# A mixture-of-experts block: eight output buffers, expert numbers read earlier, a two-part list

## The reference

```python
weights, indices = _gate(xt, gate_w)                    # 4 of 16 experts for each token
combine = jnp.einsum('tk,tke->te', weights, jax.nn.one_hot(indices, E, dtype=weights.dtype))
h1 = jnp.einsum('td,eid->tei', xt, W1)
h3 = jnp.einsum('td,eid->tei', xt, W3)
g = jax.nn.silu(h1) * h3 * combine[:, :, None]
y = jnp.einsum('tei,edi->td', g, W2)
z = jax.nn.silu(xt @ Ws1.T) * (xt @ Ws3.T) @ Ws2.T      # the shared expert
return (y + z).reshape(shape)
```

## Time and profile before

| | us |
|---|---|
| median of 3 runs (990.09, 994.32, 994.60) | 994.32 |
| the profiled execution, its own time | 992.58 |
| its span, first to last instruction | 990.8 |
| PE busy in the span | 867.0 |
| DVE busy | 732.7 |
| POOL busy | 658.6 |
| ACT busy | 573.9 |

### The profile page before, as it was taken

The page is one execution under the profiler, slowest core; times in us unless marked ns, Lnnn a source line. Parts: engine busy times, 40 slices in busy tenths (PEclk is TensorE's granted clock), DMA queues, the critical chain, the costliest instruction groups (busy, mean ns, idle before and its releaser), DMA issues.

```text
span 990.8 us, 19931 instructions
## 1 busy us (share of the span) xinstructions
PE 867.0 (88%) x6994; PEld 736.1 (74%) x6994; DVE 732.7 (74%) x1589; ACT 573.9 (58%) x1072; POOL 658.6 (66%) x625
## 2 busy tenths in 40 slices
PE   5688999999999999999999997738887899999940
PEld 5556777878878888788888786637775799999940
DVE  5777999987978788787888885585765466666648
ACT  1345777778887877887887886622321244444410
POOL 3555878978797888888788886515666555555530
PEclk9999999999999999999999999958997899999975
DMA  8661613223423235222325136233223333434337
GB/s 299 233 134 31 178 32 83 62 56 87 150 50 84 56 87 172 58 69 52 89 57 160 41 99 229 85 83 108 90 98 130 120 116 116 120 118 122 108 123 302
DMA packets 65757, 111.20 MB, mean 112 GB/s; under 512 B 16917, under 2 KB 43292, under 8 KB 63820
## 3 DMA queue, kind: packets, MB, share of 16 engines
q1 hardware_dynamic: 46905, 69.24, 26.4%
q10 hardware_dynamic: 11843, 22.84, 6.5%
q0 software_dynamic: 6912, 17.84, 4.9%
HBM read 46.06 MB, written 39.58 MB: 86 GB/s over the span
## 4 chain that ended last, share of the span: by engine, by line
PE 57%; DVE 11%; DMA 11%; POOL 11%; issue 5%; ACT 3%; SPq 0%; POOLq 0%; ACTq 0%; DVEq 0%
PE bank L691 12%; PE bank L693 10%; PE bank L692 10%; DMA slots<-h,slot_i 8%; PE bank L871 7%; PE bank L1087 7%; POOL p_lo L1927 5%; PE bank L848 4%; POOL turns L1905 2%; PE bank L1059 2%; PE bank L945 2%; DVE nmax L1261 2%; POOL slots L1983 1%; DVE qk L1241 1%; DVE turns L1235 1%
## 5 line engine op out<-in xcount | busy, mean ns | idle before, releaser
L1927 POOL TENSOR_TENSOR p_lo<-p_f,p_hi 128x512 f16<-128x512 f32 x256 | 329.5, 1299 | 46.2 <-ACT p_f L1662 45.2
L1659 ACT ACTIVATE p_hi<-bank,log_up 128x512 f16<-128x512 f32 x256 | 176.3, 689 | 108.0 <-PE bank L693 99.1
L1261 DVE TENSOR_REDUCE nmax<-bank 128x1 fp32r<-128x512 f32 x256 | 174.4, 685 | 84.4 <-PE bank L848 81.3
L1662 ACT ACTIVATE p_f<-bank,log_up 128x512 f32<-128x512 f32 x256 | 175.4, 685 | 14.7 <-POOL p_lo L1927 14.7
L871 PEld LDWEIGHTS bank<-vals,p_hi 128*128 128x128 f16 x2048 | 110.5, 98 | 59.2 <-POOL p_lo L1927 27.7
L871 PE MATMUL bank<-vals,p_hi 128*128 128x66 f16 x2048 | 138.8, 194 | 14.8 <-POOL p_lo L1927 14.5
L1905 POOL TENSOR_TENSOR turns<-turns 128x512 f32<-128x512 f32 x64 | 90.9, 1423 | 65.9 <-DVE turns L1235 65.9
L1241 DVE TENSOR_TENSOR qk<-rows_f,qk 128x512 fp32r<-128x512 f32 (+1 forms) x128 | 132.7, 1037 | 2.2
L691 PE MATMUL bank<-qk 128*128 128x512 f32 x256 | 122.2, 477 | 6.0 <-issue 4.8
L871 PE MATMUL bank<-vals,p_lo 128*128 128x66 f16 x1024 | 121.2, 193 | 0.0
L848 PE MATMUL bank<-qk 128*128 128x512 f32 x256 | 104.4, 411 | 3.6 <-DVE nmax L1261 3.2
(11 more groups left out here) (231 smaller groups left out, 2091.8 us busy)
## 6 DMA issues: line engine op xcount, KB each, us to landing
rows_f<-turns SPq DMA_DIRECT2D x64, 256.0 KB, 3.9
slots<-pad ACTq DMA_DIRECT2D x4, 2880.0 KB, 10.1
xs<-slots SPq DMA_DIRECT2D x80, 144.0 KB
w_hi<-parts SPq DMA_DIRECT2D x16, 512.0 KB, 8.4
rows_f<-kl_f SPq DMA_DIRECT2D x32, 192.0 KB, 3.0
w_raw<-in_w ACTq DMA_DIRECT2D x4, 1408.0 KB, 11.8
h_dram<-h_hl SPq DMA_DIRECT2D x3, 1024.0 KB, 4.9
qk<-lat_st SPq DMA_DIRECT2D x16, 192.0 KB, 4.3
```

The source lines that it names most:

```text
L1261: dve.tensor_reduce(nmax[:, k % MAXES:k % MAXES + 1], max_bank[q % 2][:], AX_X, ALU.max, negate=True)\
L1659: act.activation(p_hi[:, u % TB, :], score_bank[u % 2][:], ACT.Exp, bias=log_up[:, 0:1], scale=SCALE)
L1662: act.activation(p_f[:, u % 2, :], score_bank[u % 2][:], ACT.Exp, bias=log_up[:, 0:1], scale=SCALE)\
L1927: pool.tensor_tensor(p_lo[:, u % TB, :], p_f[:, u % 2, :], p_hi[:, u % TB, :], ALU.subtract).then_inc(s_pl, 1)
```

## The change

Three things.

Outputs and destinations have OUTS = 8 buffers. `ys` is now a list of eight slices: the four of before, two of `gate`'s first row, two of `zg`; `sel_i` has eight columns, and `e_put` eight semaphores. ACT and DVE wait for a landed scatter only from tile 8. The loads `xs` and `sel` keep four buffers. POOL's scatters take the same eight, and SP's last wait is for eight semaphores instead of four.

PE reads the first packed numbers ahead of shared position 14 (`t == NT - 2`), waiting there for `listed`; the waits for all weights (`w_h`, `w_l`, `ld_w2`) stand before the first routed inner product, no longer ahead of the transposes.

The list is made in two parts: `pack_experts` (behind t = 6), which subtracts one and packs, and `experts_of_tiles` (behind t = 8), which writes `own_i` and `sent_for`. `owners` goes to t = 2 and 4.

```diff
-        sel_i = sb("sel_i", [P, CYCLE], U32)
+        sel_i = sb("sel_i", [P, OUTS], U32)
...
-        ys = spare.rearrange("p (j n) -> p j n", j=CYCLE)
+        ys = [xa[:, j, :] for j in range(TB)] + [gate[:, 0, j, :] for j in range(2)] + [zg[:, j, :] for j in range(2)]
...
-            for t in range(NT):
-                shared_position(t, t % 2)
-
-
-            pe.wait_ge(listed, 1)
-            pe.wait_ge(w_h, 1 + E)
-            pe.wait_ge(w_l, 1 + E)
-            pe.wait_ge(ld_w2, 48)
-
...
+            for t in range(NT):
+                if t == NT - 2:
+                    pe.wait_ge(listed, 1)
+                    first_numbers = expert_numbers(0)
+                shared_position(t, t % 2)
...
                     expert = experts[place + 2]
+                    if m == 0:
+                        pe.wait_ge(w_h, 1 + E)
+                        pe.wait_ge(w_l, 1 + E)
+                        pe.wait_ge(ld_w2, 48)
                     pe.wait_ge(e_lo, m + 1)
...
-                if t in (3, 7):
-                    owners(t // 4)
-                if t == 11:
+                if t in (2, 4):
+                    owners(t // 2 - 1)
+                if t == 6:
+                    pack_experts()
+                if t == 8:
                     experts_of_tiles()
...
-                    if not (static(m) and m < CYCLE):
-                        dve.wait_ge(e_put[jm], 16 * over(m, CYCLE))
-                    dve.tensor_copy(sel_i[:, jm:jm + 1], sel[:, jm, 1:2]).then_inc(e_idx, 1)
+                    jo = m % OUTS
+                    if m >= OUTS:
+                        dve.wait_ge(e_put[jo], 16 * over(m, OUTS))
+                    dve.tensor_copy(sel_i[:, jo:jo + 1], sel[:, jm, 1:2]).then_inc(e_idx, 1)
...
-                    if not (static(n) and n < CYCLE):
-                        act.wait_ge(e_put[j], 16 * over(n, CYCLE))
-                    act.activation(ys[:, j], y_bank[j % 2][:, 0:D], ACT.Copy).then_inc(e_yc, 1)
+                    if n >= OUTS:
+                        act.wait_ge(e_put[n % OUTS], 16 * over(n, OUTS))
+                    act.activation(ys[n % OUTS], y_bank[j % 2][:, 0:D], ACT.Copy).then_inc(e_yc, 1)
```

More of the change, by code:

```diff
@@ L64 @@
 PACK = CYCLE + 2
-assert SLOT_TILES % CYCLE == 0 and E ** PACK <= 2 ** 24
+OUTS = 8
+assert SLOT_TILES % OUTS == 0 and SLOT_TILES % CYCLE == 0 and E ** PACK <= 2 ** 24
 R_KEEP = 0
@@ L333, in program @@
         sel = sb("sel", [P, CYCLE, 2])
-        sel_i = sb("sel_i", [P, CYCLE], U32)
+        sel_i = sb("sel_i", [P, OUTS], U32)
         h2_flat = h2[:].rearrange("p t n -> p (t n)")
         xs = sb("xs", [P, CYCLE, XW])
-        ys = spare.rearrange("p (j n) -> p j n", j=CYCLE)
+        ys = [xa[:, j, :] for j in range(TB)] + [gate[:, 0, j, :] for j in range(2)] + [zg[:, j, :] for j in range(2)]
+        assert len(ys) == OUTS
         sent_for = modT2[:].rearrange("p w c b -> p (w c b)").bitcast(I32)
@@ L400, in program @@
         ld_s = [sem(f"ld_s{j}") for j in range(CYCLE)]
-        e_put = [sem(f"e_put{j}") for j in range(CYCLE)]
+        e_put = [sem(f"e_put{j}") for j in range(OUTS)]
         ld_y = [sem(f"ld_y{j}") for j in range(PARTS_AHEAD)]
@@ L668, in _ @@
             expert_steps(sp, load_slots)
-            for j in range(CYCLE):
-                sp.wait_ge(e_put[j], 16 * (SLOT_TILES // CYCLE))
+            for j in range(OUTS):
+                sp.wait_ge(e_put[j], 16 * (SLOT_TILES // OUTS))
             sp.wait_ge(e_g, SLOT_TILES)
@@ L1090, in expert_position @@
                     mm.then_inc(e_y, 1)
-            expert_steps(pe, expert_position, expert_numbers)
+            expert_steps(pe, expert_position, lambda first: expert_numbers(first) if first else first_numbers)
         @block.vector
@@ L1454, in experts_of_tiles, with pack_experts @@
             def experts_of_tiles():
+                digits = SLOT_TILES - PACK + 1
+                src = packed_f[:, 0, :]
+                dve.tensor_copy(own_i[:, 0:digits], src).then_inc(listed, 1)
+                early = own_f[:, 0:EARLY_TILES]
+                chain(dve.tensor_scalar(early, early, float(TOPK - 1), float(PICK_SENT), ALU.min, ALU.mult))
+                chain(dve.tensor_scalar(early, early, float(PICK_SENT), None, ALU.add))
+                dve.tensor_copy(sent_for, early).then_inc(listed, 1)
+            def pack_experts():
                 chain(dve.tensor_scalar(own_f, own_f, -1.0, None, ALU.add))
@@ L1462, in experts_of_tiles @@
                     src = dst
[L1463 to L1467, removed]
             def low_weights(e):
@@ L1995, in expert_position @@
                     pool.tensor_tensor(idle[:, 1:2], mhalf[:, 0:1], mhalf[:, 0:1], ALU.add).then_inc(e_go, 1)
-                    pool.indirect_dma_start(parts, bass.IndirectOffsetOnAxis(ap=sel_i[:, j:j + 1], axis=0),
-                                            ys[:, j], None, bounds_check=last_part, oob_is_err=False).then_inc(e_put[j], 16)
+                    pool.indirect_dma_start(parts, bass.IndirectOffsetOnAxis(ap=sel_i[:, n % OUTS:n % OUTS + 1], axis=0),
+                                            ys[n % OUTS], None, bounds_check=last_part, oob_is_err=False).then_inc(e_put[n % OUTS], 16)
             expert_steps(pool, expert_position)
```

## The result

| | before | changed |
|---|---|---|
| median of 6 runs each | 994.46 us | 984.57 us |
| lowest and highest | 990.09, 996.11 | 983.14, 988.16 |
| profiled execution, its span | 992.58, 990.8 | 985.26, 983.5 |

The account below looks back on a forecast made before the run. PE was taken as the bound, with gains only around the shared stage's ends: 7.90 + 1.74 + 1.60 = 11.2 us off 992.58 gives 981.3, or 983 us against the median. Range 978 to 988.5 us, about 8 in 10.

Parts of the forecast that it names:

- Eight buffers: Start of the routed tiles: the stop at tile 4, 4.3 us idle and the rest half clock, goes whole, 7.90 us.
- 1.4 us of room: At tile 8's destination: tile 0's scatter lands 0.29 us before DVE asks, plus 1.15 us before PE notices; together 1.4 us.
- rival (1): Wait returns at tile 8 because POOL ends its scatters later relative to PE; gain 7.6, 986.7 us; chance 0.15.
- First product earlier, 1.74: Gap between shared and routed tiles: with numbers read early, the first routed inner product comes 1.74 us earlier, at 759.99.
- the clock, 1.60: After the gap before the routed tiles: the clock holds at 1.00, so 1.6 us of half rate comes back.
- The moved list, 0: Shared tiles: owners, packing and the rest moved earlier, taken as 0, with bounds of -4 and +2.5 us.
- The early value load: PE's read of the numbers at shared tile 14: price between 0 and 1.32 us, taken as 0.
- Rival (3): PE's idle 4.91 us before 746.94 ends sooner and the clock holds: up to 4 us more, 979 us; chance 0.08.
- Rival (4): Shared stage: early list work and loads slow the scatters themselves, making it slower; 996.7 us at 15 us shift; chance 0.03.
- The sum: Whole kernel: 7.90 + 1.74 + 1.60 = 11.2 us off the profiled execution's 992.58 us, giving 981.3.

Follow-up runs that it names:

- the second set: Runs on one chip beside the kernel before (median 993.09 us): the changed kernel again 982.70 us, numbers read late 982.85, owners and list at their former places 982.29.
- the old list: Changed kernel with owners behind tiles 3 and 7 and the whole list behind tile 11 again, eight buffers and early read kept: 982.29 us, ratio 0.9890.
- eight buffers alone: Kernel before with OUTS = 8 and its buffers, nothing else: 998.35 us, ratio 0.9998; run again on another chip 1000.70 us, ratio 0.9995.
- twelve buffers: Changed kernel with OUTS = 12, four more buffers in the shared expert's raw weights: 989.79 us, ratio 0.9940; run again 989.09 us, ratio 0.9946.
- both runs with DVE's idle work: Changed kernel with eight or twenty unused DVE instructions behind shared tile 12: 996.86 us, ratio 1.0008, and 1000.65 us, ratio 1.0053.
- the moves alone: Changed kernel with four buffers again, keeping the early read, the earlier owners and the list in two parts: 993.30 us, ratio 0.9963.
- the first and the third set: Two groups of runs, each sharing a chip with the kernel before, whose medians there were 996.05 us (29 runs) and 997.22 us (35 runs).
- four in flight: Changed kernel with IN_FLIGHT = 4, four slot scatters of POOL in flight instead of two: 1034.73 us, ratio 1.0371.
- the last kernel: Changed kernel with twenty DVE instructions, results unused, behind shared tile 12, some 18 us: 1000.65 us, ratio 1.0053.

## Why the prediction was right, and where it was not

**Eight buffers.** I took the stop's whole 7.90 us as gone and said it stays gone at tile 8 with 1.4 us of room. That is the step that failed: DVE asked at 768.72 us, where I had 778.44, and stood at tile 8 for 11.84 us. It was rival (1), the wait come back, but not for its reason, nor with its 3.6 us of idle PE (10.78). I had looked for POOL later; of that there was 2.4 us, 1.64 of them already at its first slot scatter (672.03 against 670.39), ahead of all that was changed. What moved was PE, 14 us earlier at the transposes (746.25 against 760.23), of which the early read is some 2.4. The rest is that the profile of before held pauses in its shared stage, which I took for a fixed part of it: PE was idle for 12.2 us of 671.00 to 757.66 before and for 3.1 us of 672.50 to 746.40 after, and busy for 74.50 and 70.77 us, at clocks of 0.93 and 0.97. The room has to be worked out for a PE without them; then tile 8 is reached long before 778 us and there is none. The right term is 4 tiles x 2.27 = 9.08 us on POOL's path, plus a small gain of clock: 9.7 between the two profiles, against 9.9 in the medians and 10.4 in the second set.

**First product earlier, 1.74, and the clock, 1.60.** Both belong to PE's path, which was not the last. There they are 1.4 us and, with the clock, 2.3 us together (3.34 taken); in the time they are nothing (982.85 against 982.70). The clock did not hold: a gap of 2.10 us was followed by 0.50 from 750 to 752 in the changed kernel, where I had argued from the earlier trace rows that it would. In the second set a gap of 2.02 us, at the same place, was followed by 0.50 in the changed kernel and by 1.00 with the old list:

```profile
747.43 0.42 PE L693 MATMUL bank<-w_hi,x_hl 128*128 x1 [2.02 <-DVE x_hl L1561]
...
748.00:750.00 2.00, 2.00 (x10) 1.94 (x9) 0.47 (x3) 0.70 (x2) 1.03 (x2) 0.50 0.77 240
```

```profile
748.54 0.42 PE L693 MATMUL bank<-w_hi,x_hl 128*128 x1 [2.02 <-DVE x_hl L1560]
...
750.00:752.00 2.00, 2.00 (x14) 1.82 (x14) 1.65 (x8) 1.11 (x4) 1.12 (x2) 1.00 0.68 201
```

So the length of the gap alone doesn't decide it, and a single row at 1.00 was no ground for 1.6 us.

**The moved list, 0.** Right within 0.8 us on PE's path, and nothing in the time, where there are no pauses. The early value load shows no idle time of PE, as taken.

**Rival (3)**, the idle 4.91 us gone, did happen, though the old list had none either, so that DVE's work there was not its cause; it brought nothing, because it was the wrong path's. **Rival (4)** did not: the scatters took 1054 ns each before and 1051 after, POOL's last one was within 2.4 us.

**The sum.** 11.2 us predicted, 7.3 between the profiles of 990.8 and 983.5 us and 9.9 between the medians. Two terms of 3.3 us that were hidden stood in it, and the first was 1.8 us too small (9.7 for 7.90), since I took the stop's cost and not the shift of the gate. Between the two profiles POOL's last slot scatter is 2.39 us later, and 9.7 less that is the 7.3. The two errors cancel in part: 11.2 less 3.34 and plus 1.8 is 9.7, beside 9.9 in the medians. That the forecast of 983 us lies 1.6 us from the measured 984.57 owes as much to this as to the mechanism.

**What stays open.** That eight buffers alone give the whole gain was not measured where the pauses are absent; each of the two moves was taken back there singly, and both profiles then hung on POOL. In the two sets with pauses eight buffers alone gave nothing. The pauses are not made by the old order: twelve buffers and both runs with DVE's idle work had them too, with the new list and the early read. Whether the moves make them fewer or cheaper (75.6 us of shared stage in the moves alone beside 91.9 in eight alone, one profile each, and the ratios above point that way), and whether the changed kernel keeps its 1% on such a chip, wasn't tried.

## What to carry to other kernels

When a wait on a buffer is released by a queue that has other work ahead of it, more buffers don't remove the wait: they move it by so many tiles, and the gain is tiles times pitch, until another path is last. Find both paths to the place and the room between them, and find out which of the idle times in the profile are the kernel's own and which only that execution's, before any of them is put into a sum. A change on the path that is not last costs nothing and brings nothing, and shows as a longer or shorter stop.

## What the runs showed of the hardware

**Pauses beside POOL's scatters.** With two indirect scatters in flight the profiles of the first and the third set show PE standing in the shared stage for up to 3.35 us at a time (1.80 in the moves alone's; stops made by the added work of DVE aside), and that of the kernel before for 4.91; DVE and ACT stand for part of it, and POOL does not. Those of the second set have no such stop of PE over 0.71 us, and the kernel before ran in 990.75 to 999.74 us there, against 986.98 to 1035.30 in the third. With four in flight PE stood for up to 28.58 us and the kernel took 1034.73. In the rows the engine that waits starts late after the one before it has ended (747.3 to 750.31), as if the signal came late. That signals are held back, and why, is argued and not shown. Loads of instructions or data beside it are not the cause in the two stretches looked at: from 747 to 752 us of the third set's eight buffers alone, and from 725 to 745 us with four in flight, every packet of the DMA queues (144 and 768) is in the queue that holds POOL's scatters. That more scatters in flight make the pauses longer is shown once, by one kernel. Three in flight was not measured.

**DVE slows POOL's scatters.** Beside the 20 instructions of DVE in the last kernel (with two inputs from SBUF, the on-chip memory, 17.97 us without a break) POOL's rows are these, from 757 to 773 us, against those of 735 to 751 us in the same execution (count, busy, mean ns, idle before and its releasers):

```profile
754.64 17.97 DVE L1523 TENSOR_TENSOR xa<-tiles_of,tab 128x680 f32<-128x680 f32 x20
```

```profile
L1998 POOL DMA_INDIRECT slots<-h,slot_i x10 | 14.8, 1483 | 3.0 <-issue 3.0
```

```profile
L1998 POOL DMA_INDIRECT slots<-h,slot_i x10 | 9.7, 971 | 5.5 <-DMA slots<-h,slot_i 4.5 <-issue 0.9
```

1483 ns for a scatter in place of 971, and POOL then no longer waits for the DMA: the pitch is some 1.8 us in place of 1.5. The Trainium skill (SBUF — State Buffer, Who interferes with whom) calls the port pair that DVE and GpSimd share an exclusive lock, and infers of this kind of DVE instruction that it doesn't hold up the generation of DMA descriptors. The trace agrees with neither in full: DVE ran on at 866 ns an instruction, and POOL made its scatters beside it, half as slow again. So the two do not shut each other out for their whole length, as the prediction had taken from the page. A scatter covered costs POOL 0.5 us of busy time, but its queue only some 0.26 us (the pitch is 17.8 us for ten in place of 15.2), since half of it fills what was a wait for the DMA. For a kernel whose gate is POOL's queue that is the price of moving such work under it.
